# An expert layer's list of slots: 64 scatters to DRAM against sums of 0/1 matrices on TensorE kept in SBUF

## The reference

```
x = x + mamba(per-subject linear(x))            # 1024 channels, 16 states, 4 taps
x = x + ffn(x @ W.T + low-rank adapter(x))      # the adapter is chosen by sequence

def ffn(x):                                     # 16 experts, 4 per token
    xt = x.reshape(-1, 512)
    cw = combine_weights(xt)                    # softmax, best 2 of 4 groups, best 4 experts, weights sum to 1
    out = zeros
    for e in range(16):
        out += cw[:, e:e + 1] * (swiglu(xt @ expert_up[e].T) @ expert_down[e].T)
    return out + swiglu(xt @ shared_up.T) @ shared_down.T
```

## Time and profile before

| | us |
|---|---|
| median of 3 runs | 2365.96 |
| lowest and highest run | 2360.68, 2367.68 |
| span of the profiled execution | 2367.9 |
| `mamba` | 0 to 1310 |
| `mix` | 1310 to 1459 |
| `shared` | 1459 to 1752 |
| `experts` | 1752 to 2368 |

### The profile page before, as it was taken

How to read it: one execution, slowest core, us unless ns; L and a number is a source line. 1 busy time by engine, 2 the same in 40 slices (tenths; PEclk the granted TensorE clock), 3 DMA queues, 4 the chain that set the end, 5 groups by cost and what they waited for, 6 DMA issues and landing times. The chain is left out here.

```text
span 2367.9 us, 31651 instructions
## 1 busy us (share of the span) xinstructions
PE 1799.2 (76%) x7956; PEld 1298.1 (55%) x7957; DVE 1644.2 (69%) x2176; ACT 732.4 (31%) x1126; POOL 1131.2 (48%) x858
## 2 busy tenths in 40 slices
PE   4778767797668867687676597993679888898888
PEld 3345434454345543455343365772558877787887
DVE  0389989999899998999894543450335655656565
ACT  1444455454545536445551122100001111111111
POOL 1167567775667656676481500017124434444443
PEclk9899878898879978798898698996789999899999
DMA  5012101120111201121010426710225455454554
GB/s 155 35 36 69 39 29 29 48 76 27 28 34 53 65 27 32 38 64 47 27 41 28 165 94 93 95 54 1 82 45 148 101 137 127 99 145 101 140 130 75
DMA packets 94383, 169.40 MB, mean 72 GB/s; under 512 B 35134, under 2 KB 40270, under 8 KB 90782
## 3 DMA queue, kind: packets, MB, share of 16 engines
q1 hardware_dynamic: 68114, 116.19, 16.8%
q0 software_dynamic: 19904, 44.92, 9.9%
q10 hardware_dynamic: 6187, 6.37, 1.0%
HBM read 261.75 MB, written 39.39 MB: 127 GB/s over the span
## 5 line engine op out<-in xcount | busy, mean ns | idle before, releaser
L789 POOL TENSOR_TENSOR dbx<-u,b_all 128x512 f32<-128x512 f32 x512 | 642.1, 1277 | 351.3 <-DVE h L687 346.0
L687 DVE TENSOR_TENSOR_SCAN h<-da,dbx 128x512 f32<-128x512 f32 x512 | 596.5, 1204 | 41.1 <-ACT da L587 41.1
L587 ACT ACTIVATE da<-delta,a_neg 128x504 f32<-128x504 f32 x512 | 347.9, 684 | 472.2 <-DVE h L687 466.5
L427 PE MATMUL hT<-ident,h 128*128 128x128 f32 x2048 | 311.4, 312 | 227.3 <-DVE h L687 226.9
L427 PEld LDWEIGHTS hT<-ident,h 128*128 128x128 f32 x2048 | 272.8, 162 | 340.2 <-issue 334.6
L700 DVE SCALAR_TENSOR_TENSOR yacc<-hT,c_now,yacc 128x512 f32<-128x512 f32 x480 | 331.6, 733 | 3.9 <-PE hT L427 3.7
L334 PE MATMUL bank<-hid,w_in 128*128 128x512 f32 x608 | 291.8, 628 | 7.0 <-ACT hid L467 7.0
L1843 POOL DMA_INDIRECT out<-y,slots_kept x76 | 129.4, 1703 | 161.4 <-DMA slots_kept<-list_scratch 95.3
L334 PEld LDWEIGHTS bank<-hid,w_in 128*128 128x128 f32 x608 | 120.9, 208 | 136.4 <-issue 128.1
L1830 POOL DMA_INDIRECT xg_kept<-x_scratch,slots_kept x72 | 83.5, 1160 | 220.8 <-PE xT_ps L1654 200.2
L1494 POOL DMA_INDIRECT list_scratch<-pairs,slot_i x64 | 62.6, 979 | 263.3 <-DVE slot_i L1445 244.2
(11 more groups left out here) (223 smaller groups left out, 3380.9 us busy)
## 6 DMA issues: line engine op xcount, KB each, us to landing
w_up_kept<-in_up_T SPq DMA_DIRECT2D x76, 1408.0 KB, 5.9
w_dn_kept<-in_dn_T SPq DMA_DIRECT2D x76, 768.0 KB, 7.3
b_all<-bt_scratch SPq DMA_DIRECT2D x128, 256.0 KB, 3.2
x_in<-in_x_pad ACTq DMA_DIRECT2D x21, 256.0 KB
res<-in_x_pad SPq DMA_DIRECT2D x20, 256.0 KB, 3.8
x_scratch<-res SPq DMA_DIRECT2D x20, 256.0 KB, 3.5
w_in<-in_in_T SPq DMA_DIRECT2D x8, 512.0 KB, 4.3
x_in<-x_scratch SPq DMA_DIRECT2D x4, 1024.0 KB, 5.5
```

The lines of the kernel that those rows point to most:

```text
L427: mm = nc.tensor.transpose(hT[t][:, d * P:(d + 1) * P], h[:, m % RING, d, t * P:(t + 1) * P], ident[:])
L587: nc.scalar.activation(out[:, :, 1:], rows[:, :, 1:], ACT.Exp, scale=a_neg[:, d, n:n + 1]) \
L687: nc.vector.tensor_tensor_scan(h[:, n % RING, i, :], da[i % RING][:], dbx[:, i, :], 0.0, ALU.mult, ALU.add).then_inc(scan_done, 1)
L789: nc.gpsimd.tensor_tensor(dbx[:, i, :], u[:, d, :], b_all[:, m % RING, :], ALU.mult) \
```

## The change

- The 64 scatters, `list_scratch`, its filling with padding and the wait for both are gone. POOL waits for `listed` and goes on with the first two tiles of slots.
- `slots()` on DVE now splits the slot number into the row in its tile (`in_tile`) and the tile (`of_tile`), turns the token number into a difference to the padding row (`token`), and keeps the weight (`weight`).
- `picks(c)` on DVE, for c from 0 to 7, builds for 8 of the 64 columns of slots (16 token tiles times 4) two operands: `at_row`, 128 x 8 x 128 with a 1 where the row number is equal to `in_tile`, and `to_list`, 128 x 8 x 2 x 85, with token and weight in the tile `of_tile` and 0 elsewhere. They have two buffers.
- `sum_picks(c)` on PE makes 8 products of `at_row` and `to_list` (fp32, 170 columns) that accumulate over all 64 in the bank that held the counts. `picks(c)` stands behind chunk c's split on DVE, `sum_picks(c)` two chunks later on PE: both lie in blocks 2 and 3.
- `list_out()` on DVE copies the sums to `lists` in SBUF, with the padding row added, in block 3. `experts` and POOL read the list from there.
- The loops over blocks on PE and ACT are written out in Python. `pad_rows` and `match` share memory with other tiles.

```diff
--- before
+++ after
@@ -1196,7 +1196,12 @@
             pool.wait_ge(ahead_lo, len(pieces))
-def shared(nc, keep, x1_d, x2_d, x2T_d, d, up_d, dn_d, list_d, out_d):
+PICKS = TILES * TOP // 8
+CHUNKS = TILES * TOP // PICKS
+BEHIND = 2
+
+
+def shared(nc, keep, x1_d, x2_d, x2T_d, d, up_d, dn_d, out_d):
     ctx = ExitStack()
@@ -1220,14 +1225,17 @@
     a = sb("sa", [P, BLK])
     a_hi = sb("sa_hi", [P, KS, BLK], F32R)
     a_lo = sb("sa_lo", [P, KS, BLK], F32R)
-    pad_list = sb("pad_list", [P, LIST_TILES, 2], I32)
-    pad_rows = sb("pad_rows", [P, DM])
+    pad_row = sb("pad_row", [P, 2], I32)
+    pad_row_f = sb("pad_row_f", [P, 1])
     tokens = sb("tokens", [P, TILES], I32)
+    tokens_f = sb("tokens_f", [P, TILES])
+    row_numbers = sb("row_numbers", [P, P])
+    list_numbers = sb("list_numbers", [P, LIST_TILES])
     strict = sb("strict", [P, P])
     ones = sb("ones", [P, P])
     restart = sb("restart", [P, EXP, TILES])
     steps = sb("steps", [P, TILES])
-    numbers = sb("numbers", [1, LIST_TILES])
+    numbers = list_numbers[0:1]
     before = sb("before", [P, EXP, TILES])
     upto = sb("upto", [P, EXP, TILES])
     more = sb("more", [P, EXP, TILES])
@@ -1236,15 +1244,24 @@
     starts = sb("starts", [P, EXP])
     place = sb("place", [P, TILES, EXP])
     best = sb("best", [P, TILES, 8])
-    match = sb("match", [P, TILES, TOP, EXP])
-    pairs = sb("pairs", [P, TILES, TOP, 2], I32)
+    match = keep["e_more"][:].rearrange("p t a b -> p (t a b)").rearrange("p (t k e) -> p t k e", t=TILES, k=TOP)
+    weight = sb("weight", [P, TILES, TOP])
     slot_i = sb("slot_i", [P, TILES, TOP], I32)
+    part_i = sb("part_i", [P, TILES, TOP], I32)
+    in_tile = sb("in_tile", [P, TILES, TOP])
+    of_tile = sb("of_tile", [P, TILES, TOP])
+    token = sb("token", [P, TILES, TOP])
+    at_row = sb("at_row", [P, RING, PICKS, P])
+    at_tile = keep["e_tie"][:].rearrange("p t a b -> p (t a b)")[:, 0:PICKS * LIST_TILES].rearrange("p (i n) -> p i n", i=PICKS)
+    to_list = sb("to_list", [P, RING, PICKS, 2, LIST_TILES])
     t_cmp = sb("t_cmp", [1, LIST_TILES, EXP])
     t_exp = sb("t_exp", [1, 1 + LIST_TILES])
     t_new = sb("t_new", [1, LIST_TILES])
     t_before = sb("t_before", [1, LIST_TILES])
     t_first = sb("t_first", [1, 1 + LIST_TILES])
     t_tmp = sb("t_tmp", [1, LIST_TILES])
+
+    pad_rows = to_list[:, 0].rearrange("p i v n -> p (i v n)")[:, 0:DM]
     gp = [ps(f"gp{i}", [P, BLK]) for i in range(RING)]
     up = [ps(f"up{i}", [P, BLK]) for i in range(RING)]
@@ -1280,7 +1298,7 @@
     x1_blk = x1_d.rearrange("(k t p) f -> k p t f", t=TB, p=P)
     out_blk = out_d[0:TOK].rearrange("(k t p) f -> k p t f", t=TB, p=P)
-    list_rows = list_d.rearrange("(i p) c -> p i c", p=P)
+    list_ps = within[:].rearrange("p t e -> p (t e)")[:, 0:2 * LIST_TILES]
     N_CONST = 7
     with ctx, nc.Block() as block:
@@ -1290,17 +1308,15 @@
                 sp.dma_start(x2T[:], x2T_d[bass.ds(j, 1)].rearrange("o p k l -> (o p) k l")).then_inc(x2_full, 16)
             load_x2(0)
-            sp.dma_start(pad_list[:], d["pad_list"]).then_inc(consts2, 16)
+            sp.dma_start(pad_row[:], d["pad_list"][:, 0, :]).then_inc(consts2, 16)
             sp.dma_start(tokens[:], d["tokens"]).then_inc(consts2, 16)
             sp.dma_start(strict[:], d["strict"]).then_inc(consts2, 16)
             sp.dma_start(ones[:], d["ones"]).then_inc(consts2, 16)
             sp.dma_start(restart[:], d["restart"]).then_inc(consts2, 16)
             sp.dma_start(steps[:], d["steps"]).then_inc(consts2, 16)
-            sp.dma_start(numbers[:], d["numbers"]).then_inc(consts2, 16)
-            sp.wait_ge(consts2, 16 * N_CONST)
-            sp.dma_start(list_rows, pad_list[:]).then_inc(pads_stored, 16)
+            sp.dma_start(list_numbers[:], d["numbers"].broadcast_to([P, LIST_TILES])).then_inc(consts2, 16)
             sp.wait_ge(pads_set, 1)
-            sp.dma_start(out_d[TOK:TOK + P], pad_rows[:]).then_inc(pads_stored, 16)
+            sp.dma_start(out_d[TOK:TOK + P], pad_rows).then_inc(pads_stored, 16)
             sp.sem_inc(out_stored, 16)
             def block_io(j, last=False):
@@ -1322,10 +1338,18 @@
             block_io(NBLK - 1, last=True)
             sp.wait_ge(ahead_in, 32)
             sp.wait_ge(out_stored, 16 * (NBLK + 1))
-            sp.wait_ge(pads_stored, 32)
+            sp.wait_ge(pads_stored, 16)
         @block.tensor
         def _(pe):
+            def sum_picks(c):
+                pe.wait_ge(picks_made, 3 * (c + 1))
+                for i in range(PICKS):
+                    mm = nc.tensor.matmul(list_ps, at_row[:, c % RING, i, :],
+                                          to_list[:, c % RING, i].rearrange("p v n -> p (v n)"),
+                                          start=(c == 0 and i == 0), stop=(c == CHUNKS - 1 and i == PICKS - 1))
+                mm.then_inc(picks_summed, 1)
+
             def expert(j):
                 for f in range(KS):
                     at = j * KS + f
@@ -1341,6 +1365,8 @@
                             mm = product(nc, bank[f % RING][:], [part[:, k, at_f] for part in (sup_hi, sup_lo)],
                                          [x2_hi[:, k, :], x2_lo[:, k, :]], k == 0, k == KM - 1)
                         mm.then_inc(full, 1)
+                    if 0 <= (j - 2) * KS + f - BEHIND < CHUNKS:
+                        sum_picks((j - 2) * KS + f - BEHIND)
                 for t in range(TB):
                     pe.wait_ge(y_out, j * TB + (t - RING + 1 if t >= RING else 0))
                     for f in range(KS):
@@ -1357,7 +1383,7 @@
             pe.wait_ge(keep["rank_step"], (NBLK + 1) * RANKS)
             nc.tensor.matmul(within[:], strict[:], sel[:], start=True, stop=True).then_inc(counts_full, 1)
             nc.tensor.matmul(totals[:], ones[:], sel[:], start=True, stop=True).then_inc(counts_full, 1)
-            with pe.Fori(2, NBLK) as j:
+            for j in range(2, NBLK):
                 expert(j)
         @block.scalar
@@ -1398,6 +1424,10 @@
                     hi_part(nc.vector, a_hi[:, f, :], a[:]).then_inc(a_split, 1)
                     dve.wait_ge(a_split, at + 1)
                     lo_part(nc.vector, a_lo[:, f, :], a[:], a_hi[:, f, :]).then_inc(a_parts, 1)
+                    if 0 <= (j - 2) * KS + f < CHUNKS:
+                        picks((j - 2) * KS + f)
+                    if (j - 2) * KS + f == CHUNKS + BEHIND:
+                        list_out()
                 if not last:
                     split_x2(j + 1)
                 dve.wait_ge(res_full, 16 * (j + 1))
@@ -1437,12 +1467,45 @@
                 for t in range(TILES):
                     step(nc.vector.max(best[:, t, :], place[:, t, :]))
-                step(nc.vector.tensor_tensor(match[:], place[:].unsqueeze(2).broadcast_to([P, TILES, TOP, EXP]),
+                step(nc.vector.tensor_tensor(match, place[:].unsqueeze(2).broadcast_to([P, TILES, TOP, EXP]),
                                              best[:, :, 0:TOP].unsqueeze(3).broadcast_to([P, TILES, TOP, EXP]), ALU.is_equal))
-                step(nc.vector.tensor_tensor(match[:], match[:], cw[:].unsqueeze(2).broadcast_to([P, TILES, TOP, EXP]), ALU.mult))
-                step(nc.vector.tensor_reduce(pairs[:, :, :, 1].bitcast(F32), match[:], AX.X, ALU.add))
-                step(nc.vector.tensor_copy(pairs[:, :, :, 0], tokens[:].unsqueeze(2).broadcast_to([P, TILES, TOP])))
-                nc.vector.tensor_scalar(slot_i[:], best[:, :, 0:TOP], -1.0, None, ALU.add).then_inc(slots_ready, 1)
+                step(nc.vector.tensor_tensor(match, match, cw[:].unsqueeze(2).broadcast_to([P, TILES, TOP, EXP]), ALU.mult))
+                step(nc.vector.tensor_reduce(weight[:], match, AX.X, ALU.add))
+                step(nc.vector.tensor_scalar(slot_i[:], best[:, :, 0:TOP], -1.0, None, ALU.add))
+                step(nc.vector.tensor_scalar(part_i[:], slot_i[:], P - 1, None, ALU.bitwise_and))
+                step(nc.vector.tensor_copy(in_tile[:], part_i[:]))
+                step(nc.vector.tensor_scalar(part_i[:], slot_i[:], P.bit_length() - 1, None, ALU.logical_shift_right))
+                step(nc.vector.tensor_copy(of_tile[:], part_i[:]))
+                step(nc.vector.tensor_scalar(tokens_f[:], tokens[:], float(-TOK), None, ALU.add))
+                step(nc.vector.tensor_tensor(token[:], tokens_f[:].unsqueeze(2).broadcast_to([P, TILES, TOP]), in_tile[:], ALU.subtract))
+                step(nc.vector.tensor_tensor_scan(row_numbers[:], ones[:], ones[:], -1.0, ALU.mult, ALU.add))
+                step(nc.vector.tensor_copy(pad_row_f[:], pad_row[:, 0:1]))
+
+            def picks(c):
+
+                def mine(x):
+                    return x.rearrange("p t k -> p (t k)")[:, c * PICKS:(c + 1) * PICKS]
+
+                by_list = [P, PICKS, LIST_TILES]
+                if c == 0:
+                    dve.wait_ge(pads_stored, 16)
+                if c >= RING:
+                    dve.wait_ge(picks_summed, c - RING + 1)
```

(48 more changed lines are left out.)

## The result

| | before | after |
|---|---|---|
| median, us | 2366.82 | 2282.48 |
| lowest and highest run | 2360.68, 2370.10 | 2280.63, 2283.54 |
| ratio of the runs, 95% interval | | 0.9642, 0.9625 to 0.9660 |
| span of the profiled execution | 2367.9 | 2280.5 |

What follows compares the result with a forecast made beforehand. No engine was always busy; a hole in block 2 of `shared`, attributed to POOL's scatters, was the loss. 69.6 + 1.3 - 19.2 - 1.6 = 50.1 us less than the 2367.9 span, 2316 us at the median; range 2303 to 2337.

Steps and rivals of the forecast that it cites:

- the list read from SBUF: In `experts`, the same 128 rows per tile read from SBUF: counted as nothing, 8 us either way for the range.
- Rival (4): More is gained because shorter list reads help `experts` by over 8 us: under 2303 us; chance 0.05.
- Scatters gone: In block 2 of `shared`, the hole in PE's work disappears with POOL's scatters: 69.6 us saved.
- rival (3): The hole comes from how engines get instructions, not the scatters, and stays: 2386 us; chance 0.06.
- Sums on PE: In blocks 2 and 3, 64 fp32 products in two passes of 0.15 us, all on the path: 19.2 us added.
- Rival (1): Weight loads are not hidden in fp32, so sums take 32 us in place of 19: 2329 us; chance 0.12.
- Picks on DVE: Eight `picks` in blocks 2 and 3, 31 us of DVE, costed at nothing because DVE has time to spare.
- Rival (2): PE and DVE run in lockstep, DVE's 31 us replacing PE's 19, plus a late end: 2331 us; chance 0.05.
- Eight steps: Ahead of block 2, eight DVE steps more and one less while PE waits: 1.6 us added.
- padding: The store that padded the list goes, so x of block 1 no longer queues behind it: 1.3 us saved.
- Order at the end: `list_out` and first gathers at the end of block 3, about 10 us, hidden behind PE's remaining 22 us.
- loops written out: Loops on PE and ACT written out: no gain, since PE's loop back edge cost nothing.

Runs made afterwards that it cites:

- the fp32r products: Kernel after with its sums in fp32r, 64 products of 256 columns in one pass replacing 170 columns in two: 2279.14 us against 2283.52.

## Why the prediction was wrong, and where it was right

- **"`experts` should take its 616 us as before"**: the step that failed. Its only term in the sum was the list read from SBUF, "I take nothing", within 8 us either way. It took 577.6, 38.6 less, and that is all of the miss: the rest of the span gave 48.8 us against 50.1. The list had next to no part in it (2.9 us at most); I had taken a stage that the diff hardly touches as fixed. The diff put 42 instructions ahead of DVE's loop, and 42 fills alone in the kernel before bring `experts` to 581.0; that was no term of the sum at all. Rival (4), "more is gained", had 0.05 and the wrong cause. The rows to ask were in the trace: 105.6 us of DVE's `aT_hi` on "issue", in 28 waits of up to 9.5 us.
- **Scatters gone, 69.6 us.** Right for the chip of that profile: block 2 fell by 56.6 us although sums (9.3 as in block 3) and a longer wait behind `slots()` (3.6 in place of 1.7) were added, so the hole was worth 67.8. On chips 4 and 5 the term is nothing or nearly so. There the change still gains (2310.3 to 2283.5, both on chip 4), but `experts` alone gains 41.7 (619.6 on chip 5, 577.9 on chip 4), by the loop's place: the first product comes at 1687.0 before (chip 5) and at 1703.8 after (chip 4), 17 us later. This sets profiles of two chips against each other. That is rival (3) in its price, a program with the sums and no hole to save, by a cause that I had not named.
- **Sums on PE, 19.2 us.** Measured 18.6; 0.145 us per pass, loads of weights hidden. Rival (1) falls. The rule of the Trainium skill (TensorE: Matmul & The Clock Gate, The mechanism) that I weighed there does not hold for the fp32r products either: 256 columns with new weights each take 0.96 / 8 = 0.12 us. An estimate by that rule would be 0.23: 0.11 for the load and half of the 0.2333 of a product with 512 columns.
- **Picks on DVE, nothing.** Right: PE waited for no picks, and DVE for PE's sums at most 0.4 us at a time, 1.5 in all. Rival (2) falls for this kernel; it is half true for the fp32r one.
- **Eight steps, 1.6; padding, 1.3.** Right: PE's wait behind `slots()` was 3.6 us (3.3 forecast); block 1 ended 1.5 us earlier.
- **Order at the end, loops written out, nothing.** Right: POOL issued the gathers of the first two tiles by 1682 us, 20 before they were wanted, and the run with loops written out alone measured 1.0007.

## What to carry over

A hardware loop of an engine can have a price that depends on where its code lies. When a diff adds or removes instructions ahead of one, look at the "issue" waits of that engine and at the packets of the instruction queue within the loop, and count the loop's place as a term with a bound; before crediting an idea with a gain in a stage that it hardly touches, pad the program back to its old place and time it. And a stall that a profile of one chip shows may be absent on the next: of a term of that size, run the kernel before on several chips.

## What the runs showed of the hardware

- A loop of 300 DVE instructions cost 37 to 43 us more or less by its place (618.1 against 581.0 on chip 1, the same list and scatters in both; 620.9 against 577.8 on chip 3). At the bad places q14 fetched 26 to 29 packets within 370 us of the loop, at the good ones none. In all it moved 0.98 MB in 120 packets, 8.2 KB each. The Trainium skill (Runtime: NRT & Kernel Launch, Instruction fetch mechanics) names such a mechanism: an engine holds a window of two blocks of its instructions, and a taken branch to a target outside it waits for a fetch. The fetches in every turn agree with that. It gives the block as 16 KiB, 256 instructions; here q14 loads 8.2 KB at a time and places 128 apart behave alike, which agree with each other and not with that block.
- Why one place is good and another bad stays open. 300 instructions touch three pieces of 128 at some places and four at others. But counted from DVE's first instruction it is the bad places (62, 72) that touch three and the good ones (104 to 126) that touch four; to be the explanation, the pieces would have to begin 24 to 55 instructions ahead of that first one, and no run shows where they begin.
- 64 indirect DMAs of POOL in a row hold PE, ACT and DVE on some chips (the given one, 1 and 6, with block 2 at 117.6 to 122.5 us where the old work stands beside them; 2, where 32 of them make it 78.0; by its time of the kernel before also 3) and not on others (5, where it took 53.3; by its times also 4). Without picks and sums beside them the hold starts 17 to 20 scatters in (21 to 25 us; five profiles), and it is absent with pauses after 8 and all but absent with pauses after 16 (10 us of small holds in block 3). In the given profile PE's products start up to 2.8 us apart as it begins (1611.23, 1612.63, 1612.87, 1614.76, 1615.48, 1616.89, 1619.71) in place of 0.23. By what way one engine's descriptors hold the others' instructions, and what differs between the chips, stays open. So does why picks and sums beside them make it milder.
